# A selective-scan kernel: scans of quads 1 to 5 start at zero, the carry goes into column 0 of their inputs, and a split moves from column 232 to 296

## The reference

```python
dA = jnp.exp(delta[..., None] * A)                          # A = -exp(A_log)
dBu = delta[..., None] * Bm[:, :, None, :] * u[..., None]
def step(h, inp):
    dA_t, dBu_t, C_t = inp
    h = dA_t * h + dBu_t
    y = jnp.einsum('ben,bn->be', h, C_t)
    return (h, y)
```

## Time and profile before

| | |
|---|---|
| time of three runs | 2513.1, 2514.06 (median), 2515.68 us |
| span of the profiled execution, first to last instruction | 2508.8 us |
| whole time of the profiled execution | not on the page; the median of the runs is 5.3 us above the span |
| busy DVE / POOL / ACT / PE | 2454.5 / 2414.8 / 2314.7 / 2142.1 us |
| DMA | 16 engines 57.9% busy with the kernel's queue, 196 GB/s |
| granted TensorE clock, mean | 0.987 of full speed |

### The profile page before, as it was taken

One profiled execution on the slowest core, in us unless ns is written; L12 is line 12 of the kernel. 1 busy time (PEld: TensorE's weight loads), 2 busy tenths in 40 slices (PEclk: granted clock), 3 DMA queues, 4 the chain that ended last, 5 costly groups with the idle time before them and its releaser, 6 DMA issues.

```text
span 2508.8 us, 35019 instructions
## 1 busy us (share of the span) xinstructions
PE 2142.1 (85%) x10314; PEld 826.0 (33%) x10314; DVE 2454.5 (98%) x2391; ACT 2314.7 (92%) x3960; POOL 2414.8 (96%) x655
## 2 busy tenths in 40 slices
PE   6788888888888888888888888888888888888878
PEld 3334434323323323323333323323323333333323
DVE  7999999999999999999999999999999999999986
ACT  5777777999999999999999999999999999999977
POOL 4999999999999999999999999999999999999991
PEclk8999999999999999999999999999999999999979
DMA  6555555556656656566566566566566565566542
GB/s 243 189 185 172 195 185 184 202 198 207 209 202 205 207 201 212 201 205 206 204 206 214 194 208 212 195 210 208 198 210 211 197 207 201 192 206 203 186 142 75
DMA packets 171388, 494.54 MB, mean 197 GB/s; under 512 B 23072, under 2 KB 44704, under 8 KB 154240
## 3 DMA queue, kind: packets, MB, share of 16 engines
q1 hardware_dynamic: 171200, 492.30, 57.9%
HBM read 400.33 MB, written 91.88 MB: 196 GB/s over the span
## 4 chain that ended last, share of the span: by engine, by line
POOL 40%; issue 40%; DVE 15%; PE 3%; ACT 1%; DMA 0%; POOLq 0%; DVEq 0%; SPq 0%; ACTq 0%
POOL R L676 20%; DVE R L1277 11%; POOL D L649 9%; POOL R L672 7%; POOL du L642 3%; DVE D L1261 2%; POOL D L658 2%; PE G L1568 1%; PE Y L1568 0%; DVE q L1357 0%; DVE dl L1287 0%; DVE G L1302 0%; DVE h L1471 0%; DVE h L1478 0%; PE Y L1645 0%
## 5 line engine op out<-in xcount | busy, mean ns | idle before, releaser
L1277 DVE TENSOR_TENSOR_SCAN R<-DA,R,D 128x512 f32<-128x512 f32 x1344 | 1630.2, 1263 | 1.0 <-ACT DA L840 1.0
L840 ACT ACTIVATE DA<-ds,kept_w 128x512 f32<-128x512 f32 x1536 | 1054.8, 688 | 139.9 <-DVE R L1277 127.1
L676 POOL TENSOR_TENSOR R<-R,Cs 128x2048 f32<-128x2048 f32 x255 | 970.9, 3819 | 4.0 <-DVE R L1277 2.6
L649 POOL TENSOR_TENSOR D<-us,Bs 128x2048 f32<-128x2048 f32 x193 | 736.9, 3818 | 8.8 <-DMA us<-lo_d 8.8
L672 POOL TENSOR_TENSOR R<-R,Cs 128x4096 f32<-128x4096 f32 x64 | 476.5, 7446 | 0.1
L1261 DVE TENSOR_TENSOR D<-us,PB 128x2048 f32<-128x2048 f32 x191 | 356.8, 1868 | 6.3 <-DMA us<-lo_d 6.3
L1645 PE MATMUL Y<-R,kept_w 128*32 128x512 f32 x2048 | 266.1, 615 | 13.9 <-POOL R L672 12.8
L1602 PE MATMUL G<-un,wcv 96*128 96x512 f32 x512 | 251.6, 614 | 29.5 <-ACT h L907 29.5
L1277 DVE TENSOR_TENSOR_SCAN R<-DA,D 128x512 f32<-128x512 f32 x192 | 221.7, 1204 | 2.1 <-ACT DA L840 2.1
L1605 PE MATMUL G<-un,wcv 96*64 96x256 f32 x1024 | 138.5, 392 | 60.1 <-ACT xq L888 58.9
L1568 PE MATMUL G<-st,kept_w 128*64 128x256 f32 (+1 forms) x384 | 108.9, 485 | 53.5 <-ACT st L802 53.5
(11 more groups left out here) (240 smaller groups left out, 3437.5 us busy)
## 6 DMA issues: line engine op xcount, KB each, us to landing
Bs<-bc_d SPq DMA_DIRECT2D x128, 512.0 KB, 5.6
us<-lo_d SPq DMA_DIRECT2D x64, 1024.0 KB, 6.3
ds<-lo_d SPq DMA_DIRECT2D x64, 1024.0 KB, 8.4
Cs<-bc_d SPq DMA_DIRECT2D x128, 512.0 KB, 4.7
us<-hi_d SPq DMA_DIRECT2D x64, 512.0 KB, 6.8
ds<-hi_d SPq DMA_DIRECT2D x64, 512.0 KB, 5.5
lo_d<-dl SPq DMA_DIRECT2D x64, 256.0 KB, 2.0
lo_d<-du SPq DMA_DIRECT2D x64, 256.0 KB, 2.0
```

Source lines behind the costliest of these rows:

```text
L649: nc.gpsimd.tensor_tensor(shaped(D[:, s % NDBU, :, :], s), low(us, s) if s in LOWS else high(us), of_states(Bs, s), ALU.mult).then_inc(don ...
L676: nc.gpsimd.tensor_tensor(shaped(R[:, s, :, 0:T], s), shaped(R[:, s, :, 1:S], s), of_states(Cs, s), ALU.mult).then_inc(hc_done.sem, 1)
L840: nc.scalar.activation(DA[j % NDA][:, :], ds[:, i, :], ACT.Exp, scale=A[:, j:j + 1]).then_inc(exp_done.sem, 1)
L1277: nc.vector.tensor_tensor_scan(R[:, s, q, 1:S], DA[j % NDA][:, :], D[:, s % NDBU, q, :], before, ALU.mult, ALU.add).then_inc(scanned.sem, 1)
```

## The change

Scans of quads 1 to 5 always start at 0.0; quad 0 keeps its start value. What the earlier chunk hands on is added to the inputs: h(0) = DA(0) * h(-1) + D(0), so DA(0) * h(-1) is added to column 0 of D. A new tile `first`, [128, 6, 4], holds it, in two parts: v = 0 for quads 1 to 3 (12 columns), v = 1 for quads 4 and 5 (8 columns). In the 56 chunks with place > 0 (`goes_on`) there is new: DVE `first_product` (A times delta's column 0) twice, ACT `first_decay` (exp of it) twice, DVE `carries` (times the last column of R) twice, DVE `take_carry` (added to D's column 0, 4 columns) for quads 1 to 5. A scan(g, s, 0) with s > 0 waits for its `take_carry`. In all 64 chunks the split of quad 3 moves from 232 to 296: DVE makes 64 columns x 4 blocks more, POOL as many less, and ACT's copy into PB is 64 columns longer.

```diff
-SPLIT = {3: 232}
+SPLIT = {3: 296}
...
+        def goes_on(k):
+            return 0 <= k <= LAST and k % CH > 0
...
+        first = sb("first", [128, QUADS, QUAD])
...
+            def first_decay(k, v):
+                act.wait_ge(first_arg.sem, first_arg.at(k, 1 + v))
+                nc.scalar.activation(first_of(v), first_of(v), ACT.Exp).then_inc(first_exp.sem, 1)
...
                 if there(g):
                     decay(g, 0, 2)
+                if goes_on(g):
+                    first_decay(g, 0)
...
                     decay(g, 3, 0)
+                if goes_on(g):
+                    first_decay(g, 1)
...
-                before = 0.0 if place(k) == 0 else R[:, s, q, T:S]
+                    if s and goes_on(k):
+                        dve.wait_ge(first_in.sem, first_in.at(k, s))
+                before = R[:, s, q, T:S] if s == 0 and goes_on(k) else 0.0
...
+            def first_product(k, v):
+                dve.wait_ge(d_in[v], count(k, 16, 16))
...
+                nc.vector.tensor_tensor(o, a, d, ALU.mult).then_inc(first_arg.sem, 1)
+
+            def carries(k, v):
+                dve.wait_ge(first_exp.sem, first_exp.at(k, 1 + v))
+                dve.wait_ge(scanned.sem, scanned.at(k - 1, (4, 6)[v] * QUAD))
+                quads = slice(1, QUAD) if v == 0 else slice(QUAD, QUADS)
+                nc.vector.tensor_tensor(first_of(v), first_of(v), R[:, quads, :, T], ALU.mult).then_inc(first_carry.sem, 1)
+
+            def take_carry(k, s):
+                dve.wait_ge(first_carry.sem, first_carry.at(k, 1 if s in LOWS else 2))
+                if s in BY_DVE:
+                    dve.wait_ge(dbu_d.sem, dbu_d.at(k, BY_DVE[s]))
+                else:
+                    dve.wait_ge(dbu_p.sem, dbu_p.at(k, BY_POOL[s]))
+                at = D[:, s % NDBU, :, 0]
+                nc.vector.tensor_tensor(at, at, first[:, s, :], ALU.add).then_inc(first_in.sem, 1)
```

More of the change, by code:

```diff
@@ L142, in at @@
                 return count(k, 1, LEAD + 1 - FIRST * CH)
+        class Continued(Progress):
+            def at(self, k, n=None):
+                return (k - batch(k) - 1) * self.per + (self.per if n is None else n)
         rows_of_R = sb("R", [128, QUADS, QUAD, S + 3])
@@ L283, in build @@
         scanned = Progress("scanned", BLOCKS)
+        first_arg, first_exp = Continued("first_arg", 2), Continued("first_exp", 2)
+        first_carry, first_in = Continued("first_carry", 2), Continued("first_in", 5)
         hc_done = Progress("hc_done", QUADS)
@@ L390, in of_states, with first_of @@
             return buf[:, HIGHS[s], :, :].unsqueeze(2).to_broadcast([128, 2, 2, T])
+        def first_of(v):
+            return first[:, 1:QUAD, :] if v == 0 else first[:, QUAD:QUADS, :]
         def pair(s):
@@ L1275, in scan @@
                     dve.wait_ge(summed.sem, summed.at(k - 1, s + 1))
-                before = 0.0 if place(k) == 0 else R[:, s, q, T:S]
+                    if s and goes_on(k):
+                        dve.wait_ge(first_in.sem, first_in.at(k, s))
+                before = R[:, s, q, T:S] if s == 0 and goes_on(k) else 0.0
                 nc.vector.tensor_tensor_scan(R[:, s, q, 1:S], DA[j % NDA][:, :], D[:, s % NDBU, q, :], before,
                                              ALU.mult, ALU.add).then_inc(scanned.sem, 1)
+            def first_product(k, v):
+                dve.wait_ge(d_in[v], count(k, 16, 16))
+                if v == 0:
+                    a = A[:, QUAD:4 * QUAD].rearrange("p (s q) -> p s q", q=QUAD)
+                    d = ds[:, 0:QUAD, 0].unsqueeze(1).to_broadcast([128, 3, QUAD])
+                    o = first_of(v)
+                else:
+                    a = A[:, 4 * QUAD:BLOCKS].rearrange("p (w i) -> p w i", i=2)
+                    d = ds[:, QUAD:QUADS, 0].unsqueeze(1).to_broadcast([128, 4, 2])
+                    o = first_of(v).rearrange("p s (w i) -> p (s w) i", i=2)
+                nc.vector.tensor_tensor(o, a, d, ALU.mult).then_inc(first_arg.sem, 1)
[8 more added lines that the diff above has]
+                    dve.wait_ge(dbu_d.sem, dbu_d.at(k, BY_DVE[s]))
+                else:
+                    dve.wait_ge(dbu_p.sem, dbu_p.at(k, BY_POOL[s]))
+                at = D[:, s % NDBU, :, 0]
+                nc.vector.tensor_tensor(at, at, first[:, s, :], ALU.add).then_inc(first_in.sem, 1)
             def delta(k, *src):
@@ L1366, in iteration @@
                     scan(g, 0, 0)
+                if goes_on(g):
+                    first_product(g, 0)
                 if there(g - 1):
@@ L1374, in iteration @@
                     scan(g, 0, 1)
+                if goes_on(g):
+                    carries(g, 0)
+                if there(g):
                     inputs(g, 1)
@@ L1378, in iteration @@
                     gate(g - 1, 1)
+                if goes_on(g):
+                    take_carry(g, 1)
                 if place(g - 10) == 0 and early(g - 10):
@@ L1383, in iteration @@
                     scan(g, 1, 0)
+                if goes_on(g):
+                    take_carry(g, 2)
+                if there(g):
                     scan(g, 1, 1)
@@ L1395, in iteration @@
                     scan(g, 2, 2)
+                if goes_on(g):
+                    first_product(g, 1)
+                if there(g):
                     inputs(g, 3)
                     scan(g, 2, 3)
+                if goes_on(g):
+                    take_carry(g, 3)
                 if there(g - 1):
@@ L1402, in iteration @@
                     scan(g, 3, 1)
+                if goes_on(g):
+                    carries(g, 1)
                 if place(g - 9) == 0 and early(g - 9):
@@ L1407, in iteration @@
                     scan(g, 3, 3)
+                if goes_on(g):
+                    take_carry(g, 4)
                 if inside(g - 10):
@@ L1416, in iteration @@
                     scan(g, 4, 2)
+                if goes_on(g):
+                    take_carry(g, 5)
+                if there(g):
                     scan(g, 4, 3)
```

## The result

The changed kernel took 3251.72 us (median of 4 runs, 3247.6 to 3251.88) against 2514.82 for the kernel before beside it: ratio 1.2936, 95% interval 1.2921 to 1.2951. The prediction said 2506, with 2490 to 2520. It missed by 746 us, and in the other direction: slower instead of faster.

The account below looks back on a forecast made before the run. DVE was taken to pace from chunk 10 on, POOL in chunks 1 to 9. Later chunks -3.7, first chunks +0.4, early chunks -4.1, chunks behind first ones -0.8: -8.2 us from 2514.06, so 2506, range 2490 to 2520.

Parts of the forecast that it names:

- Small DVE instructions: Nine new 4-to-12-column DVE instructions per chunk that goes on, at 0.095 us each: +0.855 us a chunk.
- The 97x97 step: DVE instruction of 0.23 us, next scan 0.15 us after its start; without 93 columns, the lower bound of 0.053 us.
- The upper bound: A small DVE instruction costs at most the 0.17 us that a whole 128x3 instruction takes.
- The shorter scan: DVE scans starting from 0.0 save 0.06 us each; 20 per chunk that goes on: -1.20 us.
- the fourth rival: Scan length depends on place, not start value, so the 1.20 us gain does not come: +57 us, 2563; chance 0.03.
- The split: Quad 3's inputs: 256 columns more cost DVE +0.267 us in every chunk; 256 fewer save POOL 0.454 us.
- ACT's share: ACT gets about 0.25 us more per chunk from the copy and two first_decay; put at zero, as hidden.
- The early chunks: Chunks 1 to 9, paced by POOL, each save its 0.454 us: -4.1 us.
- The 0.14 us behind a first chunk: In the chunk after a batch's first, POOL's lag goes with its 0.454 us saving: 6 x -0.14 = -0.8 us.
- The first: Rival: small DVE instructions cost their whole 0.17 us, +0.60 us a chunk, 2538 us; chance 0.16.
- Its second threshold: Above about 0.123 us per small DVE instruction, the early chunks' gain is eaten as well.
- The second: Rival: POOL is the real pacemaker throughout, so every chunk saves 0.454 us: 28.6 us less, 2485; chance 0.07.

Follow-up runs that it names:

- at 264: Kernel before the change with only quad 3's split moved from 232 to 264: 2518.04 us, ratio 1.0021.
- the version through PSUM at 296: Changed kernel with one PSUM operand in each small carry instruction on DVE, quads 0 and 1 starting from R, split 296: 2499.95 us, ratio 0.9951 to the kernel before.

## Why the prediction was wrong

**The step that failed is "Small DVE instructions".** It put 0.095 us to each, between 0.053 and 0.17. Measured, they are busy 1.6 us each. Put together, from span to span: 504 small ones +766 (806.3 less 0.08 of overlap each), 1120 scans -67, the split +17, DVE's idle time +16 (69.9 against 54.3), sum +732; the spans differ by 741.3.

Its bounds were wrong by what they were taken from. The 97x97 step reads a PSUM bank, G2, which the row prints as `G`. The 128x3 row stands in the set-up, where POOL had nothing to do. Neither shows an instruction with all tensors in SBUF beside POOL, and POOL is busy 96% of the span, so almost every new one had to meet it. The upper bound was no bound: the nearest row with POOL in it would have been POOL's own 3.8 or 7.4 us instruction.

The profile before held the hint. Each tensor_tensor and scan that DVE issues within the chunks has a tensor in PSUM: DA for the scans, PB for the inputs, Y, G. ACT even spends 572 + 572 + 353 ns a chunk on copying B into PB, though B lies in SBUF already, where POOL reads it. The runs above show a reason for it; whether the copy was put there for that reason is not shown. An edit whose operands break such a pattern needs a reason why the pattern is there before it gets a price.

**Rightly priced.** The shorter scan: 1201 against 1266 ns (the fourth rival is out). The split: +0.25 us on DVE, -0.44 on POOL. ACT's share was hidden. With a PSUM operand a small instruction takes 0.05 us from start to start, the prediction's lower bound, so at 0.095 the free case was priced too high.

**Mis-sized beside it.** The early chunks: -4.1 us was to come from POOL's 0.454. With the split alone chunks 2 to 7 take 37.16 to 37.73 us, where the kernel before has 36.91 to 37.58, and the shortest have no idle time on DVE. Chunks 1 to 9 together got 1.6 us longer (339.9 against 338.2), at 264 they got 2.6 shorter (335.6). With neither small instructions nor carry chunks 2 to 7 still vary between 36.43 and 37.82. What makes them vary is open. The 0.14 us behind a first chunk did not come with the split alone: there it grew by the full 0.26.

**The rivals.** The first had the right place, "small instructions cost more", and the price of an idle neighbour: 0.17 us, 2538. Its second threshold is a slip besides: the 8.2 us count from 0.095 and not from 0.104, so the whole gain would have been gone at 0.114 us each, not 0.123. The second, POOL as the pacemaker, is false for the kernel before (264 and 296 alone are slower), but true as soon as DVE gives back 0.1 us a chunk: the zero start at 232 ended at 2507.42 us with POOL busy for 100% of a later batch.

The sum of the parts (732 of 741) leaves little else. Left open is what lets DVE go before the end of a one-input POOL instruction.

## What to carry to other kernels

Before a DVE instruction is added beside a busy POOL, look where its tensors lie. A tensor_tensor or tensor_scalar with all of them in SBUF cost what was left of POOL's tensor_tensor, here up to 4.1 us for four columns; with one input in PSUM it cost 0.05 us. A price from a stretch where the neighbour engine is idle is no price. Where two engines are level, shorten both in one edit, or the gain stops at the other one (0.2% against 1.3% here, in the kernels without the carry).

## What the hardware showed besides

- Not every DVE instruction with its tensors in SBUF is held. In the version through PSUM at 296, with POOL in two products from 1118.65 on for 7.59 us, one takes 0.26 us; so did all five of each of the kernels before, changed and through PSUM (0.24 to 0.26 us), each beside a running POOL instruction:

```profile
1123.60 0.26 DVE L1305 BATCH_NORM_AGGREGATE mv<-bsa 128x2 f32<-128x24 f32 x1
```

- A POOL memset did not hold the two-input DVE instruction (L60, 166 ns); a one-input POOL instruction did (L59, 2207 ns), up to 1.71 us before its own end.
- TensorE's granted clock was 0.85 over the changed kernel's batch, where it was 1.00, 2.4 GHz, before: part of the time was spent at 1.2 GHz. PE was busy for 338.47 of the 423.01 us, 80%, against 86% before. It was not the cause, as DVE was busy for 420.92 of them. In the versions without the hold the clock was 1.00 again in a batch.
